# Down product and output projection with tokens on the partitions, read straight from PSUM

## The chip, the cores and the metric

The kernel runs on one core of a Trainium2 chip. The metric is the device time of one execution in microseconds, the median of the runs shown. Everything else comes from one profiled execution of the kernel before.

## The reference

The input is x, 32 sequences of 256 tokens with C = 128 channels, all in fp32. Three sublayers follow each other:

```
x = x + 0.5 * ffn(layernorm(x))
x = x + mamba(layernorm(x))
x = x + 0.5 * ffn(layernorm(x))

ffn(x):   router = x @ Wg; the top 2 of 8 experts, softmax weights w
          y  = sum over experts e of w[e] * (silu(x @ W1[e]) * (x @ W2[e])) @ W3[e]      (hidden 176)
          y += (silu(x @ Ws1) * (x @ Ws2)) @ Ws3                                         (hidden 352)
mamba(x): x_in, z = split(x @ W_in + b_in)            (256 inner channels each)
          xc = silu(causal conv of 4 taps over x_in + conv_b)
          B, C = split(xc @ W_xp + b_xp)              (16 states)
          delta = softplus(xc @ W_dt + b_dt)
          h_t = exp(delta_t * A) * h_(t-1) + delta_t * xc_t * B_t;  y_t = sum over states h_t * C_t + D * xc_t
          out = (y * silu(z)) @ W_out + b_out
          r = x + out;  return alpha * (r - mean(r)) / (std(r) + 1e-6) + beta
```

The residual inside `mamba` is its own input, that is the normalised x, so this normalised x is needed twice: as the input of `W_in` and, later, as the residual of the output projection.

## The kernel before, in words

Work goes in groups of two sequences, 512 tokens (TG), four tiles of 128 (TILES); there are G = 16 groups. A software pipeline of iterations k = -2 to 17 works on three groups at a time: in iteration k the first FFN runs for group k + 2, the projections that feed the scan for group k + 1, the scan itself for group k, the end of the mamba layer and the routing of the second FFN for group k - 1, and the second FFN for group k - 2. Each iteration has 32 slots. Every engine walks through the same slots in order and runs what the tables put there, so an instruction that waits holds back everything behind it on its engine. Hand-overs are semaphores.

In each slot: the scan of one of 16 states takes two slots. On even slots TensorE spreads a row of B over the partitions (`row_b`, L1008), VectorE scans (L868) and GpSimd multiplies by a row of C (L569); on odd slots VectorE makes the next input term (`input_term`, L834), which needs the `row_b` of the next even slot. The FFNs have NCHUNK = 14 units of 128 hidden channels each: the second one (f = 1) starts them in slots 0 to 13, the first one (f = 0) in slots 14 to 27. A unit is the up products `h1` and `h2` on TensorE (L1030, L1048), Silu on ScalarE (L680), the gate on VectorE one slot later (L860), for expert units another product on GpSimd (L521), and the down product four slots later (L1043) into the bank `ps_y`. The down product has `down_w` as the stationary operand and 512 tokens moving, so the channels come out on the partitions, `ps_y[c, token]`. The residual `xres` is kept with tokens on the partitions. So the result makes a detour: `y0`/`y1` copies `ps_y` to `yT` on ScalarE (L730), `yT0`/`yT1` transposes it in four blocks into the shared bank `ps_m` (L1079), and `addy0`/`addy1` adds half of it to `xres` on VectorE (L926). The first down product of the next FFN (slot 18 for f = 0, slot 4 for f = 1) waits until `ps_y` is taken (`y_taken`, L1042).

The output projection takes the same way: `outproj` (L1110) gives channels on the partitions, ScalarE adds `b_out` and copies to `oT` (L733), `outT` transposes, and `resid` (L961) adds it to `rtok` on VectorE. `rtok` holds the normalised residual: `x1n` (L699 to L706) computes it a second time on ScalarE, one iteration after `norm2` computed the same values for the projection. `stats3`, `ln_norm` and three GpSimd operations then finish the layer (`mamba_added`, L557).

All these small steps share one bank, `ps_m`. The order of their turns is the order in `PLAN` (L54): `claim` (L985) lets TensorE write only when the step before has been taken, and the taker is the engine that reads it: ScalarE for transposes of x, `in0` to `in3`, `dt0`, `dt1`, `bT`, `cT`, `wT`; VectorE for `logits`, `xproj`, `yT`, `outT`.

Other steps that matter: `gate_y` (L945) finishes the scan's output on VectorE; `weights0`/`weights1` (L908) turn the router's choice into weights, starting with `den` (L912); `wT0`/`wT1` transpose them, and SP writes them to memory and spreads them over the partitions again (`store_w`, `rows_w`). `delta` (L928) needs the softplus that ScalarE makes of `dt0`, `dt1` with Abs, Exp and Ln; `bparts` (L935) splits B into three bf16 parts. `SP_PLAN` (L64) is the same table for the DMA queue of SP.

## Time and profile before

| | |
|---|---|
| time, three runs | 2228.62, 2232.82, 2250.01 us; median 2232.82 |
| the profiled execution | 2241.29 us, its span 2239.5 us |
| mean granted clock of TensorE | 0.887 |
| TensorE busy | 1794.9 us, 80% of the span |
| VectorE busy | 1639.6 us, 73% |
| ScalarE busy | 1535.3 us, 69% |
| GpSimd busy | 1441.3 us, 64% |
| chain that ended last | PE 43%, ACT 21%, DVE 17%, issue 12%, POOL 3% |

PE is TensorE, PEld its weight loads, DVE VectorE, ACT ScalarE, POOL GpSimd; L numbers are lines of the kernel. A busy TensorE is not one at its full rate: the same instruction takes twice as long when the granted clock is at its lower level. Busy times of two instructions that follow each other can overlap by some hundredths of a microsecond; for the pace, read from start to start. An fp32 matmul shows as two records.

### The profile page before, as it was taken

To read this page: it belongs to the slowest core of one execution; us is meant where nothing else is said; L and a number is where in the kernel's file an instruction comes from. 1 tells how busy PE (TensorE), PEld (TensorE's weight loads), DVE (VectorE), ACT (ScalarE), POOL (GpSimd) and SP (SyncE) were. 2 spreads that over 40 slices of the span, in tenths; PEclk is the share of its full clock that TensorE was granted. 3 is DMA by queue.
4 is the path that set the end of the run, shared out by engine and by line. 5 is a ranking of instruction groups with operands and counts; after the bars stand their busy time and mean duration, and the time that the engine had idled before them with its cause. 6 is when DMAs were issued, how large, how long until landed. Compare 5 with 4: busy or idle time off the path is not lost.

```text
span 2239.5 us, 22836 instructions
## 1 busy us (share of the span) xinstructions
PE 1794.9 (80%) x4674; PEld 804.4 (36%) x4674; DVE 1639.6 (73%) x2505; ACT 1535.3 (69%) x2083; POOL 1441.3 (64%) x1286
## 2 busy tenths in 40 slices
PE   3878587979888888887888798788888878885577
PEld 1433233434334333333433343333333433332233
DVE  2257878687786878878687877878778786879742
ACT  1257587777778767786876778687677867776522
POOL 3346676666667675776767666676766676676753
PEclk9989788989898898998989898898989889897698
DMA  4117565555556555555555654655556555557642
GB/s 130 45 55 178 119 164 130 144 133 143 127 142 153 130 135 134 152 132 151 152 137 129 152 143 127 151 147 140 130 131 159 131 145 138 133 122 173 150 111 61
DMA packets 119129, 300.05 MB, mean 134 GB/s; under 512 B 19184, under 2 KB 40400, under 8 KB 104656
## 3 DMA queue, kind: packets, MB, share of 16 engines
q0 software_dynamic: 18432, 125.84, 28.1%
q1 hardware_dynamic: 92672, 168.88, 24.2%
q10 hardware_dynamic: 7888, 4.09, 0.7%
q14 instruction: 123, 1.01, 0.1%
q8 instruction: 14, 0.23, 0.0%
HBM read 167.67 MB, written 5.24 MB: 77 GB/s over the span
## 4 chain that ended last, share of the span: by engine, by line
PE 43%; ACT 21%; DVE 17%; issue 12%; POOL 3%; ACTq 1%; DMA 1%; DVEq 0%; POOLq 0%
PE ps_y L1043 9%; PE ps_h2a L1048 6%; DVE hist L868 5%; PE ps_m L1003 5%; ACT L680 5%; PE ps_h1a L1030 4%; PE ps_h1b L1030 4%; ACT L657 4%; PE ps_h2b L1048 4%; DVE den L912 3%; ACT decay L657 3%; ACT silu L680 2%; DVE yacc L950 2%; PE ps_m L1110 2%; DVE ps_db L834 2%
## 5 line engine op out<-in xcount | busy, mean ns | idle before, releaser
L569 POOL TENSOR_TENSOR prod<-hist,crow 128x1024 f32<-128x1024 f32 x224 | 556.0, 2482 | 371.8 <-DVE hist L868 368.0
L1043 PE MATMUL ps_y<-gated,down_w 128*128 128x512 f32 (+1 forms) x896 | 517.6, 664 | 101.3 <-POOL gated L521 63.2
L868 DVE TENSOR_TENSOR_SCAN hist<-decay,ps_db 128x1024 f32<-128x1024 f32 x256 | 583.2, 2278 | 13.8 <-issue 11.3
L521 POOL TENSOR_TENSOR gated<-gated,silu 128x512 f32<-128x512 f32 x352 | 476.3, 1416 | 138.1 <-DVE gated L860 108.4
L834 DVE TENSOR_TENSOR ps_db<-du,ps_db 128x1024 f32<-128x1024 f32 x256 | 313.7, 1225 | 319.1 <-PE ps_db L1012 318.8
L657 ACT ACTIVATE decay<-delta,a_neg 128x510 f32<-128x510 f32 x512 | 338.1, 711 | 2.6
L1048 PE MATMUL ps_h2a<-xnT,up_w 128*128 128x512 f32 (+1 forms) x448 | 253.2, 649 | 53.3 <-DVE gated L860 53.3
L680 ACT ACT_TABLE_LOAD x227 | 291.2, 1283 | 5.5 <-issue 0.7
L1043 PEld LDWEIGHTS ps_y<-gated,down_w 128*128 128x128 f32 (+1 forms) x896 | 180.3, 209 | 319.3 <-issue 218.0
L1030 PE MATMUL ps_h1a<-xnT,up_w 128*128 128x512 f32 (+1 forms) x448 | 248.0, 636 | 49.7 <-ACT silu L680 48.8
L657 ACT ACT_TABLE_LOAD x217 | 278.4, 1283 | 3.8
L1030 PE MATMUL ps_h1b<-xnT,up_w 128*128 128x512 f32 x448 | 240.1, 618 | 38.8 <-ACT silu L680 38.5
L1048 PE MATMUL ps_h2b<-xnT,up_w 128*128 128x512 f32 x448 | 235.9, 609 | 0.0
L680 ACT ACTIVATE silu<-ps_h1a 128x512 f32<-128x512 f32 (+1 forms) x224 | 132.8, 593 | 57.6 <-PE ps_h1a L1030 57.3
L680 ACT ACTIVATE silu<-ps_h1b 128x512 f32<-128x512 f32 x224 | 133.8, 597 | 48.3 <-PE ps_h1b L1030 43.1
L1012 PE MATMUL ps_db<-bT,sel_b 96*128 96x512 bf16 x256 | 108.3, 423 | 69.4 <-DVE hist L868 69.3
L860 DVE TENSOR_TENSOR gated<-ps_h2b,wrow 128x512 f32<-128x512 f32 x192 | 131.2, 683 | 41.2 <-PE ps_h2b L1048 41.2
L860 DVE TENSOR_TENSOR gated<-ps_h2a,wrow 128x512 f32<-128x512 f32 x160 | 108.5, 678 | 68.2 <-PE ps_h2a L1048 64.8
L1048 PEld LDWEIGHTS ps_h2a<-xnT,up_w 128*128 128x128 f32 (+1 forms) x448 | 89.0, 202 | 183.0 <-issue 109.8
L718 ACT ACTIVATE bounce<-ps_m 8x512 f32<-8x512 f32 x32 | 18.8, 587 | 184.7 <-PE ps_m L993 184.7
L1030 PEld LDWEIGHTS ps_h1b<-xnT,up_w 128*128 128x128 f32 x448 | 81.4, 196 | 134.7 <-issue 69.2
L1003 PE MATMUL ps_m<-xnT,w_conv 128*128 128x512 f32 (+3 forms) x256 | 121.9, 621 | 6.6 <-DVE rtok L961 4.2
(137 smaller groups left out, 2242.5 us busy)
## 6 DMA issues: line engine op xcount, KB each, us to landing
yacc<-prod POOLq DMA_DIRECT2D x112, 1024.0 KB, 9.0
crow<-c_rows SPq DMA_DIRECT2D x128, 512.0 KB, 4.2
wrow<-w_rows SPq DMA_DIRECT2D x320, 128.0 KB, 3.6
wrow<-w_rows SPq DMA_DIRECT2D x64, 224.0 KB, 3.2
wrow<-w_rows SPq DMA_DIRECT2D x64, 192.0 KB, 3.6
wrow<-w_rows SPq DMA_DIRECT2D x64, 160.0 KB, 3.4
yacc<-yacc POOLq DMA_DIRECT2D x16, 512.0 KB, 6.2
wrow<-w_rows SPq DMA_DIRECT2D x64, 96.0 KB, 3.3
```

What stands on the lines that cost most here:

```text
L521: nc.gpsimd.tensor_tensor(gated[:, pos % NGATE, :], gated[:, pos % NGATE, :], silu[:, (pos + NCHUNK * f_parity(k, f)) % NSILU, :], ALU.mul ...
L569: nc.gpsimd.tensor_tensor(prod[:, (pair - 1 + odd) % 2, s % 2, :, :], hist[:, s % 2, :, :], c_all, ALU.mult).then_inc(prod_done, 1)
L657: ins = nc.scalar.activation(decay[:, s % NA, half, :, 1:LEN], d[:, :, 1:LEN], ACT.Exp, scale=a_neg[:, half, s:s + 1])
L680: nc.scalar.activation(silu[0:r, (pos + NCHUNK * f_parity(k, f)) % NSILU, :], ps_h1[pos % 2][0:r, :], ACT.Silu).then_inc(silu_done, 1)
L834: nc.vector.tensor_tensor(ps_db[:].rearrange("p (h t) -> p h t", h=HALVES), du[par][:], ps_db[:, TG:2 * TG].unsqueeze(1).to_broadcast([P, ...
L860: nc.vector.tensor_tensor(gated[0:r, pos % NGATE, :], ps_h2[pos % 2][0:r, :], factor, ALU.mult).then_inc(h2_taken, 1)
L868: nc.vector.tensor_tensor_scan(hist[:, s % 2, :, :].rearrange("p h t -> p (h t)"), decay[:, s % NA, :, :, :].rearrange("p h b t -> p (h b ...
L1003: nc.tensor.matmul(acc[:, :, late:LEN], w_conv[:, tap, half * P:(half + 1) * P], now[:, :, 0:LEN - late], start=(tap == PAD), stop=False)
L1012: nc.tensor.matmul(ps_db[:, TG:2 * TG], sel_b[:, s, :], bT[par][:], start=True, stop=True).then_inc(b_full, 1)
L1030: nc.tensor.matmul(ps_h1[pos % 2][0:r, :], up_w[:, 0, j * P:j * P + r], xnT[f][:], start=True, stop=True).then_inc(h1_full, 1)
L1043: nc.tensor.matmul(ps_y[:], down_w[0:rd, jd, :], gated[0:rd, posd % NGATE, :], start=(posd == 0), stop=(posd == NCHUNK - 1)).then_inc(down ...
L1048: nc.tensor.matmul(ps_h2[pos % 2][0:r, :], up_w[:, 1, j * P:j * P + r], xnT[f][:], start=True, stop=True).then_inc(h2_full, 1)
```

## The change

The operands of two products are swapped. In the down product each of the four token tiles of `gated` is the stationary operand, and the 128 columns of `down_w` move; the result has tokens on the partitions. `addy` reads `ps_y` itself and sets `y_taken`; `y0`, `y1`, `yT0`, `yT1` and `yT` are gone. The output projection is turned in the same way, with the bias brought in first by a matmul of a row of ones with `b_out`; `resid` reads its result, `outT` and `oT` are gone. `norm2` writes into one of two kept tiles, `x1n[2]`, and SP copies it to `rtok` with a DMA in slot 17 (`keep_x1n`); the second computation is gone. Most steps of `PLAN` and some of `SP_PLAN` get new slots.

```diff
-        0: ["stats0", "y0"], 1: ["yT0", "x1n"], 2: ["addy0", "norm0"], 3: ["stats2", "fold"], 4: ["xT0"],
-        5: ["logits0", "norm2"], 6: ["route0", "gate_y"], 7: ["xT2"], 8: ["weights0", "outproj"], 9: ["in0"],
-        10: ["wT0"], 11: ["outT"], 12: ["resid"], 13: ["in1", "stats3"], 14: ["in2"],
-        15: ["in3", "ln_norm"], 17: ["y1"], 18: ["dt0", "stats1"], 19: ["dt1"], 20: ["yT1", "norm1"],
-        21: ["addy1"], 22: ["xproj", "delta"], 23: ["bparts"], 24: ["xT1"], 25: ["logits1"], 26: ["route1"],
-        27: ["cT"], 28: ["bT", "weights1"], 30: ["wT1"],
+        0: ["stats0", "addy0"], 1: ["stats2"], 2: ["norm0"], 3: ["norm2", "fold"], 4: ["xT0"], 5: ["logits0"],
+        6: ["route0", "xT2"], 7: ["gate_y"], 8: ["weights0"], 9: ["outproj"], 10: ["resid", "in0", "stats3"],
+        11: ["wT0"], 12: ["in1"], 13: ["in2"], 14: ["in3", "ln_norm"], 16: ["dt0"], 17: ["dt1", "addy1", "stats1"],
+        19: ["xproj", "norm1"], 20: ["delta", "bparts"], 21: ["xT1"], 22: ["logits1"], 23: ["route1"],
+        24: ["cT"], 25: ["weights1"], 26: ["bT"], 28: ["wT1"],
     }
     UP1, UP0, BACK = 0, 14, 4
 
     SP_PLAN = {
         0: ["c1"], 3: ["c2"], 4: ["w1:4"], 5: ["w1:5"], 6: ["w1:6"], 7: ["c3", "w1:7"], 8: ["w1:8"], 9: ["w1:9"],
-        10: ["w1:10"], 11: ["store_w0", "c4"], 12: ["w0:0"], 13: ["w0:1"], 14: ["w0:2"], 15: ["w0:3", "c5"],
-        18: ["w0:4"], 19: ["c6", "w0:5"], 20: ["w0:6"], 21: ["w0:7"], 22: ["store_x", "w0:8"], 23: ["c7", "w0:9"],
-        24: ["w0:10"], 28: ["next_c0"], 30: ["store_w1", "w1:0", "w1:1", "w1:2", "w1:3"],
+        10: ["w1:10"], 11: ["c4"], 12: ["store_w0"], 13: ["w0:0", "w0:1"], 14: ["w0:2"], 15: ["w0:3", "c5"],
+        17: ["keep_x1n"], 18: ["w0:4"], 19: ["c6", "w0:5"], 20: ["w0:6"], 21: ["store_x", "w0:7"], 22: ["w0:8"],
+        23: ["c7", "w0:9"], 24: ["w0:10"], 28: ["next_c0"], 29: ["store_w1", "w1:0", "w1:1", "w1:2", "w1:3"],
     }
 
...
-    MISC_LEAD = ["yT0", "xT2", "in0", "in1", "in2", "in3", "dt0", "dt1", "xproj", "cT", "bT"]
-    MISC_TAIL = ["outproj", "outT", "xT1", "logits1", "wT1"]
-    MISC_LAST = ["yT1"]
+    MISC_LEAD = ["xT2", "in0", "in1", "in2", "in3", "dt0", "dt1", "xproj", "cT", "bT"]
+    MISC_TAIL = ["outproj", "xT1", "logits1", "wT1"]
...
+        b_out_r = sb("b_out_r", [1, C])
+        ones_r = sb("ones_r", [1, P])
...
-        xn = [sb(f"xn{f}", [P, TILES, C]) for f in range(2)]
-        xn = [xn[0], xn[0], xn[1]]
+        xn = sb("xn", [P, TILES, C])
+        x1n = [sb(f"x1n{i}", [P, TILES, C]) for i in range(2)]
...
@@ -369,7 +366,7 @@
 
             def store(g, slot, first, k):
 
-                sp.wait_ge(misc_taken, turn(k, "yT1"))
+                sp.wait_ge(y_taken, ffn_no(k, 1) + 1)
...
+                        elif step == "keep_x1n" and scans(k):
+                            sp.wait_ge(norm_ready[2], k + 1)
+                            if tail(k):
+                                sp.wait_ge(mamba_added, k)
+                            sp.dma_start(rtok[:], x1n[odd][:]).then_inc(x1n_ready, 16)
...
                         elif step == "stats2" and lead(k):
                             if tail(k):
-                                pool.wait_ge(x1n_ready, k)
+                                pool.wait_ge(norm_ready[2], k)
                             scale_and_bias(k, step, mv1[:, nxt, :, :], ln_eps, rstd1[:, nxt, :],
                                            nbias1[:, nxt, :], k + 2)
...
+                const(b_out_r[:], b_out.rearrange("(o c) -> o c", o=1))
...
-                            normalise(xn[0], xres[:, entering, :, :], nbias[0], rstd[0]).then_inc(norm_ready[0], 1)
+                            normalise(xn, xres[:, entering, :, :], nbias[0], rstd[0]).then_inc(norm_ready[0], 1)
                         elif step == "norm1" and tail(k):
                             plain_wait()
                             act.wait_ge(nbias_ready[1], k)
-                            normalise(xn[1], xres[:, behind, :, :], nbias[1], rstd[1]).then_inc(norm_ready[1], 1)
+                            normalise(xn, xres[:, behind, :, :], nbias[1], rstd[1]).then_inc(norm_ready[1], 1)
                         elif step == "norm2" and lead(k):
                             plain_wait()
+                            if tail(k):
+                                act.wait_ge(x1n_ready, 16 * k)
                             act.wait_ge(nbias_ready[2], k + 2)
-                            normalise(xn[2], xres[:, ahead, :, :], nbias1[:, nxt, :], rstd1[:, nxt, :]
+                            normalise(x1n[nxt], xres[:, ahead, :, :], nbias1[:, nxt, :], rstd1[:, nxt, :]
                                       ).then_inc(norm_ready[2], 1)
-                        elif step == "x1n" and tail(k):
-
-                            plain_wait()
-                            act.wait_ge(nbias_ready[2], k)
-                            if not isinstance(k, int) or k > 1:
-                                act.wait_ge(mamba_added, k - 1)
-                            normalise(rtok, xres[:, behind, :, :], nbias1[:, nxt, :], rstd1[:, nxt, :]
-                                      ).then_inc(x1n_ready, 1)
...
-                        elif step == "y0" and lead(k) or step == "y1" and last(k):
-                            f = int(step[1])
-                            act.wait_ge(down_done, fcount(k if f else k - 1, f, NCHUNK, NCHUNK))
-                            nc.scalar.activation(yT[:], ps_y[:], ACT.Copy).then_inc(y_taken, 1)
-                        elif step == "outproj" and tail(k):
-                            take(k, step)
-                            nc.scalar.activation(oT[:], ps_m[:], ACT.Identity,
-                                                 bias=b_out_c[:, 0:1]).then_inc(misc_taken, 1)
                         elif step in ("in0", "in1") and lead(k):
                             half = int(step[2])
+                            if tail(k):
+                                act.wait_ge(yg_ready, k)
                             take(k, step)
                             nc.scalar.activation(xconv[nxt][:, half, :], ps_m[:], ACT.Silu,
                                                  bias=b_conv[:, half:half + 1]).then_inc(misc_taken, 1)
@@ -880,7 +871,7 @@
                             statistics(xres[:, behind, :, :], 1, mv[1], stats_no(k, 1))
...
-                            dve.wait_ge(misc_taken, turn(k, "yT0"))
+                            dve.wait_ge(y_taken, ffn_no(k - 1, 0) + 1)
                             statistics(xres[:, ahead, :, :], 2, mv1[:, nxt, :, :], stats_no(k, 2))
...
                         elif step == "addy0" and lead(k) or step == "addy1" and last(k):
                             f = int(step[4])
-                            dve.wait_ge(misc_full, turn(k, f"yT{f}"))
+                            dve.wait_ge(down_done, fcount(k if f else k - 1, f, NCHUNK, NCHUNK))
                             xr = xres[:, oldest if f else ahead, :, :].rearrange("p t c -> p (t c)")
-                            nc.vector.scalar_tensor_tensor(xr, ps_m[:], 0.5, xr, ALU.mult, ALU.add
-                                                           ).then_inc(misc_taken, 1)
+                            nc.vector.scalar_tensor_tensor(xr, ps_y[:], 0.5, xr, ALU.mult, ALU.add
+                                                           ).then_inc(y_taken, 1)
...
                         elif step == "resid" and tail(k):
-                            dve.wait_ge(x1n_ready, k)
-                            dve.wait_ge(misc_full, turn(k, "outT"))
+                            dve.wait_ge(x1n_ready, 16 * k)
+                            dve.wait_ge(misc_full, turn(k, "outproj"))
                             r2 = rtok[:].rearrange("p t c -> p (t c)")
                             nc.vector.tensor_tensor(r2, r2, ps_m[:], ALU.add).then_inc(misc_taken, 1)
                         elif step == "stats3" and tail(k):
                             plain_wait()
-                            dve.wait_ge(misc_taken, turn(k, "outT"))
+                            dve.wait_ge(misc_taken, turn(k, "outproj"))
                             statistics(rtok, 3, mvr, stats_no(k, 3))
...
                         if posd == 0 and (not isinstance(k, int) or k > -2):
                             pe.wait_ge(y_taken, ffn_no(k, fd))
-                        nc.tensor.matmul(ps_y[:], down_w[0:rd, jd, :], gated[0:rd, posd % NGATE, :], start=(posd == 0),
-                                         stop=(posd == NCHUNK - 1)).then_inc(down_done, 1)
+                        for t in range(TILES):
+                            ins = nc.tensor.matmul(ps_y[:, t * C:(t + 1) * C],
+                                                   gated[0:rd, posd % NGATE, t * P:(t + 1) * P], down_w[0:rd, jd, :],
+                                                   start=(posd == 0 and t == 0),
+                                                   stop=(posd == NCHUNK - 1 and t == TILES - 1))
+                        ins.then_inc(down_done, 1)
...
                             pe.wait_ge(norm_ready[f], (k + 3, k, k + 2)[f])
                             claim(k, step)
-                            to_rows(xn[f], P, ident, ps_m).then_inc(misc_full, 1)
+                            to_rows(x1n[nxt] if f == 2 else xn, P, ident, ps_m).then_inc(misc_full, 1)
...
-                        elif step == "yT0" and lead(k) or step == "yT1" and last(k):
-                            f = int(step[2])
-                            pe.wait_ge(y_taken, ffn_no(k if f else k - 1, f) + 1)
-                            claim(k, step)
-                            to_rows(yT, P, ident, ps_m).then_inc(misc_full, 1)
...
                         elif step == "outproj" and tail(k):
                             pe.wait_ge(yg_ready, k)
                             claim(k, step)
-                            for half in range(HALVES):
-                                ins = nc.tensor.matmul(ps_m[:], w_out[:, half, :], yacc[nxt][:, 0, half, :],
-                                                       start=(half == 0), stop=(half == HALVES - 1))
+                            nc.tensor.matmul(ps_m[:].rearrange("p (t c) -> p t c", t=TILES), ones_r[:],
+                                             b_out_r[:].unsqueeze(1).to_broadcast([1, TILES, C]), start=True,
+                                             stop=False)
+                            for t in range(TILES):
+                                for half in range(HALVES):
+                                    ins = nc.tensor.matmul(ps_m[:, t * C:(t + 1) * C],
+                                                           yacc[nxt][:, 0, half, t * P:(t + 1) * P],
+                                                           w_out[:, half, :], start=False,
+                                                           stop=(t == TILES - 1 and half == HALVES - 1))
                             ins.then_inc(misc_full, 1)
-                        elif step == "outT" and tail(k):
-                            claim(k, step)
-                            to_rows(oT, P, ident, ps_m).then_inc(misc_full, 1)
```

## Rows read from the trace of the kernel before

**Rows 1.** Window view of one iteration: busy us per engine (instructions), clock, DMA.
```profile
1018.99:1149.62 130.63, 110.29 (x294) 49.44 (x293) 103.83 (x156) 99.98 (x135) 89.94 (x80) 0.90 0.55 142
```

**Rows 2.** TensorE's timeline, same iteration: start, us, instructions; idle before and its releaser.
```profile
1023.43 0.65 PE L993 MATMUL ps_m<-ident,yT 128*128 128x128 f32 x4 [0.76 <-ACT yT L730]
...
1027.91 1.35 PE L1030 MATMUL ps_h1b<-xnT,up_w 128*128 128x512 f32 x2 [1.89 <-ACT silu L680]
...
1051.10 1.13 PE L1048 MATMUL ps_h2a<-xnT,up_w 128*128 128x512 f32 x2 [3.68 <-DVE gated L860]
...
1056.35 3.58 PE L1003 MATMUL ps_m<-xnT,w_conv 128*128 128x512 f32 x8
...
1092.49 1.10 PE L1043 MATMUL ps_y<-gated,down_w 128*128 128x512 f32 x2 [3.17 <-ACT yT L730]
1093.43 1.80 PE L1048 MATMUL ps_h2a<-xnT,up_w 128*128 128x512 f32 x2
1095.02 2.84 PE L1093 MATMUL ps_m<-xconv,w_dt 128*128 128x512 f32 x4
...
1111.57 2.08 PE L1030 MATMUL ps_h1a<-xnT,up_w 128*128 128x512 f32 x2 [3.19 <-ACT silu L680]
...
1139.80 2.08 PE L1043 MATMUL ps_y<-gated,down_w 128*128 128x512 f32 x2 [3.75 <-POOL gated L521]
```

**Rows 3.** Summary of TensorE's waits, whole run: us, times, longest.
```profile
PE ps_y L1043 <- ACT yT L730: 38.0, 12, 3.2
```

**Rows 4.** TensorE's timeline, back to back at full clock.
```profile
1044.88 0.60 PE L993 MATMUL ps_m<-ident,xn 128*128 128x128 f32 x4
1045.32 0.38 PE L1012 MATMUL ps_db<-bT,sel_b 96*128 96x512 bf16 x1
1045.54 1.02 PE L1030 MATMUL ps_h1a<-xnT,up_w 128*128 128x512 f32 x2
1046.39 1.02 PE L1043 MATMUL ps_y<-gated,down_w 128*128 128x512 f32 x2
```

**Rows 5.** TensorE's timeline, an x-projection at full clock.
```profile
217.41 1.87 PE L1102 MATMUL ps_m<-w_xp,xconv 128*128 128x32 f32 x16
219.12 1.10 PE L1030 MATMUL ps_h1b<-xnT,up_w 128*128 128x512 f32 x2
```

**Rows 6.** Groups by line and shape: busy us, mean ns, idle before, releaser.
```profile
L868 DVE TENSOR_TENSOR_SCAN hist<-decay,ps_db 128x1024 f32<-128x1024 f32 x256 | 583.2, 2278 | 13.8 <-issue 11.3
...
L834 DVE TENSOR_TENSOR ps_db<-du,ps_db 128x1024 f32<-128x1024 f32 x256 | 313.7, 1225 | 319.1 <-PE ps_db L1012 318.8
...
L860 DVE TENSOR_TENSOR gated<-ps_h2b,wrow 128x512 f32<-128x512 f32 x192 | 131.2, 683 | 41.2 <-PE ps_h2b L1048 41.2
...
L912 DVE TENSOR_SCALAR den<-edrop 128x4 f32<-128x4 f32 x32 | 73.4, 2294 | 1.0 <-POOL edrop L542 1.0
...
L933 DVE TENSOR_TENSOR du<-delta,xconv 128x1024 f32<-128x1024 f32 x16 | 50.1, 3130 | 0.5
...
L914 DVE TENSOR_TENSOR prob<-edrop,prob 128x4 f32<-128x4 f32 x32 | 36.1, 1128 | 1.1
...
L819 DVE CAST bparts<-bc 128x64 bf16<-128x64 f32 x16 | 25.2, 1577 | 0.5
...
L644 ACT ACTIVATE rtok<-xres,nbiasx,rstdx 128x128 f32 x48 | 19.6, 483 | 0.0
...
L730 ACT ACTIVATE yT<-ps_y 128x512 f32<-128x512 f32 x32 | 18.9, 591 | 19.9 <-PE ps_y L1043 19.9
```

**Rows 7.** VectorE's timeline, same iteration.
```profile
1027.96 0.69 DVE L860 TENSOR_TENSOR gated<-ps_h2b,silu 128x512 f32<-128x512 f32 x1 [2.18 <-ACT silu L680]
...
1039.92 1.23 DVE L834 TENSOR_TENSOR ps_db<-du,ps_db 128x1024 f32<-128x1024 f32 x1 [2.21 <-PE ps_db L1012]
...
1139.00 5.51 DVE L912 TENSOR_SCALAR den<-edrop 128x4 f32<-128x4 f32 x1
```

**Rows 8.** DMA issues: KB each, median us to landing.
```profile
out<-xres SPq DMA_DIRECT2D x16, 256.0 KB, 2.9
```

9 lines of the change are left out of this document (3 added, 6 removed).

## The prediction

> **What bounds the kernel now.** I read the window view of one whole iteration first [rows 1]. It lasts 130.6 us and is one of the 12 (k = 2 to 13) that hold every step. TensorE is busy for 110 of it, VectorE for 104, ScalarE for 100, so three engines are nearly full and a freed engine soon meets the next. The granted clock is 0.90, so TensorE spends part of the time at the lower level. Next I read TensorE's own timeline through that iteration [rows 2]: where it waits, and for whom. It waits for ScalarE in the head (0.76 before `yT0`'s transposes, 1.89 before an up matmul), for VectorE in slot 8 (3.68), not at all from there to slot 18, then for the eviction `yT` (3.17), then for a Silu behind the Exp/Ln chain (3.19), and in the tail for GpSimd (3.75). These six come to 16.4 us. The summary of waits has the `yT` one 12 times, 38.0 us in all [rows 3], so every full iteration has it.
>
> A wait costs more than its length. After 3.19 us of idling the next two-record matmul takes 2.08 instead of 1.02 [rows 2, 4], the lower of the two levels (1.2 instead of 2.4 GHz); after 3.17 us the next but one takes 1.80, and the four records of dt0 2.84, where at the full rate four last 4 x 0.43 + 0.16 = 1.88.
>
> **The matmuls turned round.** Before, a down unit is two records of 512 moving columns, 0.86 from start to start (1045.54 to 1046.39 is such a pair [rows 4]). After, it is four tiles of two records, each with 128 moving columns of `down_w` and its own load of 128 columns of `gated`: eight loads and eight short matmuls. Columns moved are the same, 0.86 us. The question is whether the loads hide. The nearest rows: the x-projection already has this form with 32 columns, and its 16 records take 1.71 us (217.41 to 219.12, and the pair behind them lasts 1.10, so this is the full clock [rows 5]), 107 ns each, so a 128-column fp32 load passes in at most 107 ns. The fp32 transposes load 128 columns and move 128, and four take 0.44 (1044.88 to 1045.32 [rows 4]), 110 ns each, so load and movement overlap there. Hence 8 x 107 to 8 x 110 = 0.86 to 0.88: I take no change, upper bound load and movement in series, 8 x 214 = 1.71 us, lower bound 0.86.
>
> The Trainium skill speaks against this change: its page "TensorE: Matmul & The Clock Gate" (Back-to-back issue gap) gives about 81 ns for each matmul of 128 columns in a stream of load and matmul pairs, against 56 ns without loads. By that ratio, an estimate, a down unit would take 1.24 us, 10.7 us more in an iteration. The transposes do not show it (110 ns with a 128-column load), but they are not quite the same instruction.
>
> The output projection goes from four records (1.72) to sixteen of 128 columns (16 x 107 = 1.71) plus the bias matmul of 512 columns (0.86). Removed are `outT`, `yT0`, `yT1`, 0.44 each. TensorE's net is -0.5 us an iteration, bounds -0.5 and +25.
>
> **What leaves the other queues.** ScalarE loses three evictions of a bank, two `yT` at 0.59 and `oT` (taken alike), and `x1n`, four instructions of 0.48 [rows 6]: 1.8 + 1.9 = 3.7 us. VectorE loses nothing: the residual add reads the other bank at the same size. The copy of x1n is one 256 KB transfer on SP in slot 17; the output transfer of the same size takes 2.9 us [rows 8]. Its readers come in slot 10 of the next iteration, so I cost it at nothing. It waits for `mamba_added`, and behind it on SP stand `w0:4` and `c6`, wanted from slot 19; before, GpSimd's last add ends before VectorE's statistics in slot 18 need it, so that cover holds. Were it late by one 2.9 us transfer, the rows of weights would be too.
>
> **Now the schedule, stretch by stretch,** in us per iteration.
> (a) Slot 18. `y_taken` now comes from VectorE's add in slot 17 (as long as a gate, 0.68 [rows 6]), with dt1 (1.72) and an up matmul (0.86) of TensorE's between: no wait. Gain 3.17, and the slow passage behind it (1.80 for 1.02, 2.84 for 1.88 [rows 2]), 1.7: **-4.9**. Bounds 0 and -4.9. The Silu wait of 3.19 stays: its chain of Abs, Exp, Ln and their table loads moves two slots but keeps its length.
> (b) Head, slots 0 to 8. ScalarE's `yT` and `x1n` go, 0.59 + 1.93 = 2.5 us, and `wT1` reaches it two slots sooner; its two waits are worth 2.7, and smaller ones follow. VectorE is late next: in this stretch it is idle only 2.18 + 2.21 = 4.4 [rows 7]. I take **-3.3**, bounds 0 and -4.4. The move of `gate_y` behind the gate of slot 7 lies inside this.
> (c) Tail. `den` of weights1 stood in slot 28 for 5.51 us [rows 7] on four elements a partition, so nearly all of it is a wait inside the instruction; no up unit covers it there, and scan 15, the first weights of the next iteration and the clock all wait. It moves to slot 25. Scan 14 to the next row_b then is GpSimd's and VectorE's pace: **-5.3**, bounds -2 and -6.
> (d) TensorE's content: **-0.5**.
> (e) Slot 10. `resid` and `in0` now share slot and bank, so the convolution waits for VectorE's add, which stands behind input term 1.23, gate 0.68 and scan 2.28, and is as long as a gate [rows 6]: 4.9 after row_b, 4.6 with overlaps. TensorE's own slot is 0.22 + 3 x 0.86 = 2.8. That alone is a wait of 1.8; and without in0 in slot 9 (3.58 [rows 2]) TensorE comes 3.6 sooner, less 0.1, while VectorE is still held by `gate_y` and weights0. Wait 5.3, slow passage 0.8 (3.17 us lowered the clock, 3.68 did not): **+6.1**, bounds +1.8 and +9.
> (f) Slots 20 to 22. du (3.1) and the parts of B (the first cast alone 1.6 [rows 6]) stand in one slot with a scan, 7.0 us of VectorE against 2.8 of TensorE; xT1 waits for `bc` and the gates stand behind: **+3.2**, bounds 0 and +5.
> (g) Slot 25. weights1 costs on average 2.3 + 1.1 for `den` and `prob` [rows 6] and 1.0 for the rest, 4.4 us of VectorE; some 2.4 has slack: **+2.0**, bounds 0 and +4.4.
> Similar waits in slot 6 (xT2 behind route0, 2 us) fall where VectorE sets the pace anyway: 0.
>
> Sum -14.0 + 11.3 = **-2.7 us**. The sixteen iterations that scan, twelve of them full, give -43; the four at the ends lose a hop of 0.59 + 0.44 and two handovers, 1.5 each, -6. The profiled execution took 2241.3 us (span 2239.5), 8.5 above the median of the three runs; 2241.3 - 49 = 2192, or **2184** on the median's scale.
>
> **Rivals.**
> *New waits do not bind* (0.20). VectorE runs ahead as ScalarE feeds it sooner, and (e) to (g) cost about half, 6, with the rest as is: -14 + 6 = -8, x 16 and the -6 of the ends, 2099. For it: ScalarE, busy 100 of 130.6, has its idle time in the tail behind `wT1`, and that moves; against: VectorE too has only 4.4 idle in the head.
> *Nothing is left* (0.15). Either (e) to (g) eat all, or a short record takes 120 ns: 28 x 8 x 13 ns = +2.9 an iteration, 2233.
> *Slower: in0 behind resid* (0.13). The price is in slot 10. If the clock falls in the wait and stays down over in0, that is 5.3 + 3.7, and (a) gives back only its 3.17: -2.7 + 2.9 + 1.7 + some 1.5 more in (f) = +3.4, 16 x 3.4 = +54, 2285. It decides as soon as TensorE stands more than about 5 us there in most iterations.
> *Slower: loads not hidden* (0.07). If a load and a movement of 107 ns follow each other, 28 x 0.85 = +24 an iteration, +380, near 2570; if they overlap by half, near 2380. The 110 ns of the transposes speak against it [rows 4]. (By the ratio of the Trainium skill's page it would be 16 x 10.7 = +171, near 2355.)
> *The forecast* (0.45): small gain, 2150 to 2215.
>
> **Numbers.** A measurement of this kernel tells about 1% (22 us) from no change. Faster by over 1% means below 2210: 0.20 + nearly all of 0.45 less 0.04, 0.61. Within 1%: 0.15 + 0.04, 0.19. Slower: 0.13 + 0.07, 0.20. The range leaves out the 0.07, half of the 0.13 and a quarter of the 0.20: 2090 to 2275.
>
> **What would show it.** Down records near 107 ns at full clock, and 0.86 for a unit, or the loads rival is true. No wait at slot 18 and no `den` of 5 us in the tail, for (a) and (c). A wait of 4 to 6 us before the first convolution, released by `rtok`, for (e); if it is under 2, the second case holds. ScalarE 3.7 us less busy an iteration. A mean clock at or above 0.89; below 0.87 the slot 10 rival holds. Most likely wrong are the sizes of (e) and (f), because they depend on how far VectorE is behind.

## The result and the profile after

The kernel after takes 2350.11 us (median of four runs, 2347.12 to 2353.02) against 2234.21 (2228.62 to 2250.01) of the kernel before: a ratio of 1.0507, interval 1.0451 to 1.0562. It is 116 us slower, where 2184 was forecast, and lies outside the range. The profiled execution took 2351.95 us, its mean granted clock is 0.882.

The page of the kernel after (span 2350.2 us): busy time by engine, a queue that carries instructions, and the chain that ended last.

```profile
PE 1850.3 (79%) x7394; PEld 1087.3 (46%) x7394; DVE 1647.8 (70%) x2505; ACT 1484.2 (63%) x1973; POOL 1437.7 (61%) x1287
...
q8 instruction: 67, 1.10, 0.2%
...
PE 39%; DVE 25%; issue 14%; ACT 9%; POOL 9%; DMA 2%; ACTq 1%; DVEq 1%; POOLq 0%
```

ScalarE is 51 us less busy than before, 3.2 an iteration, nearly the 3.7 that the prediction counted. VectorE and GpSimd are busy as before to within 8 us. So the work did leave, and the time still grew. TensorE is busy 55 us longer, in part at the lower clock and in part with the slightly longer down units (13 us, priced under e8), and the other 55 us of the longer span are its waits. The queue q8 (packets, MB, share) had 14 packets and 0.23 MB before.

The window view of two iterations, which answers to [rows 1] (window, length, busy us of PE, PEld, DVE, ACT, POOL with instructions, clock, DMA share, GB/s):

```profile
922.35:1058.69 136.34, 113.72 (x463) 67.27 (x463) 102.08 (x155) 96.20 (x126) 87.74 (x77) 0.91 0.52 130
1058.69:1199.67 140.98, 114.56 (x463) 67.41 (x462) 105.85 (x158) 96.34 (x126) 91.14 (x82) 0.90 0.55 141
```

Both are longer than the 130.6 of before, at 0.91 and 0.90 of the clock against 0.90. They differ from each other because the program's loop runs over two iterations, and one of the two has the wait at the loop's end (4.67, told of below; the difference is 4.64).

TensorE's timeline, a full-clock passage of the first and then the second of these iterations, which answers to [rows 2, 4] (start, us, instructions; idle before and its releaser):

```profile
1008.00 1.05 PE L1035 MATMUL ps_y<-down_w,gated 128*128 128x128 f32 x8
1008.89 1.02 PE L1043 MATMUL ps_h2a<-xnT,up_w 128*128 128x512 f32 x2
...
1092.56 1.12 PE L1043 MATMUL ps_h2b<-xnT,up_w 128*128 128x512 f32 x2 [2.89 <-DVE gated L851]
1093.61 2.07 PE L1099 MATMUL ps_m<-b_out_r,ones_r 1*128 1x512 f32 x2
1095.61 3.78 PE L1104 MATMUL ps_m<-w_out,yacc 128*128 128x128 f32 x16
...
1104.51 3.68 PE L994 MATMUL ps_m<-xnT,w_conv 128*128 128x512 f32 x8 [1.72 <-DVE rtok L952]
...
1137.34 1.55 PE L1035 MATMUL ps_y<-down_w,gated 128*128 128x128 f32 x8 [3.67 <-POOL gated L524]
1138.68 1.91 PE L1043 MATMUL ps_h2b<-xnT,up_w 128*128 128x512 f32 x2
1140.38 2.37 PE L1083 MATMUL ps_m<-xconv,w_dt 128*128 128x512 f32 x4
1142.59 0.38 PE L1003 MATMUL ps_db<-bT,sel_b 96*128 96x512 bf16 x1
```

Four things are to be seen. A turned down unit takes 0.89 from start to start at full clock (1008.00 to 1008.89), so the loads hide. The wait for `yT` (3.17 before) is gone, but in slot 17, one slot ahead of where it was, stands one of 3.67 for GpSimd's last gate product. The output projection runs at the lower clock, 3.78 us for its sixteen records, behind a wait of 2.89 for VectorE in slot 8, where 3.68 stood before with a projection at full clock behind it. And the convolution waits 1.72 for `resid`, not 5.3.

The summary of waits of the kernel after (engine, tile, line, releaser: us, times, longest), which answers to [rows 3]:

```profile
PE ps_y L1035 <- POOL gated L524: 126.6, 59, 7.1
...
PE ps_h2b L1043 <- DVE gated L851: 64.9, 29, 2.9
PE ps_m L994 <- DVE rtok L952: 27.7, 14, 4.2
...
PE ps_h1a L1021 <- issue: 18.2, 5, 4.7
```

Before, the first of these was 63.2 us in 21 waits; now it is 63.4 us more in 38 more waits. The last line is of another kind and is told of below.

Why is GpSimd late? Its own timeline around slots 14 to 17 of the same iteration, kernel after:

```profile
1127.99 1.26 POOL L553 TENSOR_TENSOR rtok<-rtok,alpha_b 128x512 f32<-128x512 f32 x1 [7.09 <-ACT rtok L647]
...
1132.07 2.35 POOL L572 TENSOR_TENSOR prod<-hist,crow 128x1024 f32<-128x1024 f32 x1
...
1135.09 0.89 POOL L589 DMA_DIRECT2D yacc<-prod  x1 [0.24 <-issue]
1135.70 1.58 POOL L524 TENSOR_TENSOR gated<-gated,silu 128x512 f32<-128x512 f32 x1
```

And the same stretch of the kernel before, with the gate product first:

```profile
1083.82 1.59 POOL L521 TENSOR_TENSOR gated<-gated,silu 128x512 f32<-128x512 f32 x1
1086.90 1.27 POOL L550 TENSOR_TENSOR rtok<-rtok,alpha_b 128x512 f32<-128x512 f32 x1 [1.49 <-ACT rtok L644]
```

`ln_norm` moved from slot 15 to 14. In each slot GpSimd's program has the gate product first, then the steps of the table, then the product of the scan, so a step that moves from slot 15 to 14 passes ahead of slot 15's gate product. GpSimd now comes to it too soon, stands 7.09 us for ScalarE's part of it, then owes three operations, the product of slot 14's scan and a DMA issue, 7.71 us together (1127.99 to 1135.70), and only then the gate product for which TensorE has waited 3.67. Over the run GpSimd waits 106.1 us for this release in the kernel after, 20.7 before. TensorE's wait of this slot is there in twelve iterations (3.67 to 3.70 each), and a thirteenth has 7.13.

### The profile page after: what moved, and what is told of

Same layout as the page of the kernel before. It is cut to its first block, busy times and chain, and to the rows that moved or that the text cites. A ratio compares the mean times of both kernels' runs of the same rounds, so it can differ in the third digit from the quotient of the medians.

```text
span 2350.2 us, 28083 instructions
## 1 busy us (share of the span) xinstructions
PE 1850.3 (79%) x7394; PEld 1087.3 (46%) x7394; DVE 1647.8 (70%) x2505; ACT 1484.2 (63%) x1973; POOL 1437.7 (61%) x1287
## 4 chain that ended last, share of the span: by engine, by line
PE 39%; DVE 25%; issue 14%; ACT 9%; POOL 9%; DMA 2%; ACTq 1%; DVEq 1%; POOLq 0%
DVE hist L859 10%; PE ps_y L1035 8%; PE ps_m L994 5%; PE ps_h2b L1043 5%; PE ps_h1a L1021 4%; POOL gated L524 4%; POOL prod L572 4%; PE ps_h1b L1021 3%; DVE ps_db L825 3%; PE ps_h2a L1043 3%; PE ps_m L1104 2%; DVE gated L851 2%; DVE yacc L941 2%; ACT L683 2%; ACT L660 2%
## 5 line engine op out<-in xcount | busy, mean ns | idle before, releaser
L572 POOL TENSOR_TENSOR prod<-hist,crow 128x1024 f32<-128x1024 f32 x224 | 549.3, 2452 | 327.3 <-DVE hist L859 326.1
L1035 PEld LDWEIGHTS ps_y<-down_w,gated 128*128 128x128 f32 (+1 forms) x3584 | 506.7, 208 | 347.8 <-POOL gated L524 192.7
L1035 PE MATMUL ps_y<-down_w,gated 128*128 128x128 f32 (+1 forms) x3584 | 528.3, 296 | 128.6 <-POOL gated L524 126.6
L524 POOL TENSOR_TENSOR gated<-gated,silu 128x512 f32<-128x512 f32 x352 | 487.4, 1452 | 137.9 <-DVE gated L851 127.3
L1043 PE MATMUL ps_h2b<-xnT,up_w 128*128 128x512 f32 x448 | 250.5, 643 | 65.0 <-DVE gated L851 64.9
L1021 PE MATMUL ps_h1a<-xnT,up_w 128*128 128x512 f32 (+1 forms) x448 | 254.6, 652 | 32.8 <-issue 18.2
L1043 PE MATMUL ps_h2a<-xnT,up_w 128*128 128x512 f32 (+1 forms) x448 | 241.9, 623 | 7.3 <-DVE gated L851 6.3
L994 PE MATMUL ps_m<-xnT,w_conv 128*128 128x512 f32 (+3 forms) x256 | 130.3, 657 | 33.5 <-DVE rtok L952 27.7
L1021 PEld LDWEIGHTS ps_h1a<-xnT,up_w 128*128 128x128 f32 (+1 forms) x448 | 89.4, 205 | 91.7 <-issue 63.6
L729 ACT ACTIVATE xconv<-ps_m,b_conv 128x512 f32<-128x512 f32 x32 | 22.0, 687 | 160.8 <-PE ps_m L996 160.8
```

The source lines that it names most:

```text
L524: nc.gpsimd.tensor_tensor(gated[:, pos % NGATE, :], gated[:, pos % NGATE, :], silu[:, (pos + NCHUNK * f_parity(k, f)) % NSILU, :], ALU.mul ...
L572: nc.gpsimd.tensor_tensor(prod[:, (pair - 1 + odd) % 2, s % 2, :, :], hist[:, s % 2, :, :], c_all, ALU.mult).then_inc(prod_done, 1)
L994: nc.tensor.matmul(acc[:, :, late:LEN], w_conv[:, tap, half * P:(half + 1) * P], now[:, :, 0:LEN - late], start=(tap == PAD), stop=False)
L1021: nc.tensor.matmul(ps_h1[pos % 2][0:r, :], up_w[:, 0, j * P:j * P + r], xnT[f][:], start=True, stop=True).then_inc(h1_full, 1)
L1035: ins = nc.tensor.matmul(ps_y[:, t * C:(t + 1) * C], gated[0:rd, posd % NGATE, t * P:(t + 1) * P], down_w[0:rd, jd, :], start=(posd == 0 a ...
L1043: nc.tensor.matmul(ps_h2[pos % 2][0:r, :], up_w[:, 1, j * P:j * P + r], xnT[f][:], start=True, stop=True).then_inc(h2_full, 1)
```

## The experiments

The theories at the start: the loss comes from the two steps that moved in slots 9 to 15 (`ln_norm`, and `resid` with `in0`); or it comes from the short records of the turned products; or from the new head or the new tail. Each experiment changes one of these. All times are medians against the kernel before on the same chip, which took 2238.64 us beside e1 to e4, 2232.81 beside e5 to e8, 2235.12 beside e9 to e11 and 2246.2 beside e12. Two kernels measured beside different ones are therefore known against each other to a few microseconds only; where it matters, the ratios to before are given too.

**The products alone, in the old slots (e1_old_slots).** The kernel after with the slots of before (the cut shows the table of before, then e1's): `addy0` in 0, `addy1` in 17, `outproj` in 11, the detours left out, the copy of x1n in slot 17.

```diff
-        0: ["stats0", "y0"], 1: ["yT0", "x1n"], 2: ["addy0", "norm0"], ... 8: ["weights0", "outproj"],
-        ... 11: ["outT"], 12: ["resid"], ... 17: ["y1"], ... 20: ["yT1", "norm1"], 21: ["addy1"],
+        0: ["stats0", "addy0"], 2: ["norm0"], ... 8: ["weights0"],
+        ... 11: ["outproj"], 12: ["resid"], ... 17: ["addy1"], ... 20: ["norm1"],
```

> The changed kernel's products, kept x1n and copy, in the slots of the kernel before: only addy0 moves to slot 0, addy1 to slot 17 and the output projection to slot 11, where outT stood. Placement theory (the slots 9 to 17 of the new table lose the time): no wait of 3.7 us for GpSimd before the last down product, no wait of the first convolution for rtok; some 138 us per iteration fall to 128 to 131, the time is 2190 to 2250 us. Product theory (eight short records with their own loads lose it, through the loads or the longer loop body): still above 2300 us, because all short records stay.

Measured 2191.63 us, ratio 0.9796 (0.975 to 0.9842), 47 us faster than before, at the lower end of the range that was expected (2190 to 2250). So turning the products, with the x1n kept, is no loss. All that the kernel after loses, 159 us from here, lies in its tables of slots, `PLAN` and `SP_PLAN`. TensorE's timeline of this kernel at slots 17 and 18 and further on:

```profile
1069.32 1.88 PE L1125 MATMUL ps_m<-xconv,w_dt 128*128 128x512 f32 x4
1071.04 1.02 PE L1063 MATMUL ps_h1b<-xnT,up_w 128*128 128x512 f32 x2
1071.89 1.05 PE L1077 MATMUL ps_y<-down_w,gated 128*128 128x128 f32 x8
...
1084.91 1.35 PE L1063 MATMUL ps_h1a<-xnT,up_w 128*128 128x512 f32 x2 [3.25 <-ACT silu L725]
```

No wait of 3 us is left there; the Silu wait behind it stays (3.25 here, 3.19 in [rows 2]), as forecast.

**The down product wide again, rest as after (e2_wide_down).** This kernel leaves out what the wide form needs: `ps_y` holds channels on the partitions and is added to `xres` as it stands, without transposes. It serves to price the records.

```diff
-                        for t in range(TILES):
-                            ins = nc.tensor.matmul(ps_y[:, t * C:(t + 1) * C],
-                                                   gated[0:rd, posd % NGATE, t * P:(t + 1) * P], down_w[0:rd, jd, :],
-                                                   start=(posd == 0 and t == 0),
-                                                   stop=(posd == NCHUNK - 1 and t == TILES - 1))
-                        ins.then_inc(down_done, 1)
+                        nc.tensor.matmul(ps_y[:], down_w[0:rd, jd, :], gated[0:rd, posd % NGATE, :], start=(posd == 0),
+                                         stop=(posd == NCHUNK - 1)).then_inc(down_done, 1)
```

> The changed kernel, but each down unit is again one matmul of 512 moving columns (two records), with down_w stationary; ps_y then holds channels on the partitions and is added to xres untransposed, so the output is not the reference's. Everything else, slots too, is as in the changed kernel. Placement theory: only the 0.03 us per unit (0.89 against 0.86 us, 13 us in all) and the waits of 2.4 to 4.7 us at the end of a pass of TensorE's loop (5 seen, with the slow passage some 25 us) go: 2305 to 2330 us. Product theory: most of the 116 us goes, below 2270 us.

Measured 2339.4 us, 1.0468 (1.0421 to 1.0515): 11 us less than after, where 20 to 45 were expected. The short records are not the cause of the 116 us. They cost less here than the 30 us that e8 finds for them; where the rest went was not followed.

**ln_norm back in slot 15 (e3_lnnorm_15).**

```diff
-        11: ["wT0"], 12: ["in1"], 13: ["in2"], 14: ["in3", "ln_norm"], 16: ["dt0"], ...
+        11: ["wT0"], 12: ["in1"], 13: ["in2"], 14: ["in3"], 15: ["ln_norm"], 16: ["dt0"], ...
```

> The changed kernel with one step moved: ln_norm from slot 14 to slot 15, where it stood before, so that GpSimd's product for the last down unit (issued in slot 15 ahead of the table's steps) does not stand behind its three operations. Placement theory: TensorE's wait of 3.67 us before the down product of slot 17 and the slow passage behind it go or shrink to under 1 us: 3 to 5 us per iteration, 2270 to 2305 us. Product theory: within 1% of 2350 us.

Measured 2274.1 us, 1.016 (1.0111 to 1.021): 76 us less than after, for one step moved by one slot. Its GpSimd timeline, where the gate product comes first again, and TensorE's down product of slot 17, without a wait:

```profile
1109.28 1.59 POOL L546 TENSOR_TENSOR gated<-gated,silu 128x512 f32<-128x512 f32 x1
1111.86 1.27 POOL L575 TENSOR_TENSOR rtok<-rtok,alpha_b 128x512 f32<-128x512 f32 x1 [0.99 <-ACT rtok L669]
```

```profile
1112.82 1.05 PE L1057 MATMUL ps_y<-down_w,gated 128*128 128x128 f32 x8
```

In its summary of TensorE's waits, the one for GpSimd's gate product is back to the size of before (63.2 us in 21 waits):

```profile
PE ps_y L1057 <- POOL gated L546: 62.6, 34, 5.1
```

**The order of slots 9 to 15 as before (e4_resid_12).** `in0` in 9, `wT0` 10, `outproj` 11, `resid` 12, `in1` and `stats3` 13, `in2` 14, `in3` and `ln_norm` 15; the rest as after.

```diff
-        9: ["outproj"], 10: ["resid", "in0", "stats3"], 11: ["wT0"], 12: ["in1"], 13: ["in2"], 14: ["in3", "ln_norm"],
+        9: ["in0"], 10: ["wT0"], 11: ["outproj"], 12: ["resid"], 13: ["in1", "stats3"], 14: ["in2"],
+        15: ["in3", "ln_norm"],
```

> The changed kernel with only the slots 9 to 15 laid out as before: in0 9, wT0 10, outproj 11, resid 12, in1 and stats3 13, in2 14, in3 and ln_norm 15; the head (0 to 8) and the tail (16 to 28) keep the new slots. Placement theory: the first convolution no longer waits for rtok and the wait for GpSimd in slot 17 is gone; 2250 to 2290 us, and what is still above the old-slot kernel is what the new head and tail cost. Product theory: above 2320 us.

Measured 2210.51 us, 0.9881 (0.9837 to 0.9925): 64 us less than e3, 140 less than after, and below the range that was expected (2250 to 2290). The wait for `rtok` is down from 25.4 us in 14 waits (e3) to 4.2 in one.

**The place of stats3 (e5_stats3_13).** e3 with `stats3` in slot 13. In e3 and in the kernel after GpSimd stands in slot 10 for these statistics (5.20 us in the kernel after), ahead of its products; this run asks whether that costs the 64 us.

```diff
-        10: ["resid", "in0", "stats3"], 11: ["wT0"], 12: ["in1"], 13: ["in2"],
+        10: ["resid", "in0"], 11: ["wT0"], 12: ["in1"], 13: ["in2", "stats3"],
```

> The kernel of e3_lnnorm_15 (2274 us) with only stats3 moved from slot 10 to slot 13, so that GpSimd no longer stands 5.2 us in slot 10 waiting for these statistics in front of the products of the scan and the gates; resid and in0 stay together in slot 10. Theory A (the convolution behind the residual add, and the slow passage after the wait of 2.9 us before the output projection, cost the rest): no change, 2265 to 2285 us. Theory B (GpSimd's early wait costs it): most of the 64 us down to e4_resid_12 goes, 2215 to 2240 us.

Measured 2278.55 us, 1.0203 (1.0144 to 1.0263), as e3. GpSimd's wait for these statistics falls from 88.7 us in the whole run (e3) to 2.6, and the time does not follow: it is not that.

**The tail alone (e6_new_tail).** e1 with slots 16 to 31 of the new table, and SP's from slot 21.

```diff
-        17: ["addy1"], 18: ["dt0", "stats1"], 19: ["dt1"], 20: ["norm1"], 22: ["xproj", "delta"], 23: ["bparts"],
-        24: ["xT1"], 25: ["logits1"], 26: ["route1"], 27: ["cT"], 28: ["bT", "weights1"], 30: ["wT1"],
+        16: ["dt0"], 17: ["dt1", "addy1", "stats1"], 19: ["xproj", "norm1"], 20: ["delta", "bparts"], 21: ["xT1"],
+        22: ["logits1"], 23: ["route1"], 24: ["cT"], 25: ["weights1"], 26: ["bT"], 28: ["wT1"],
```

> The kernel of e1_old_slots (2192 us) with slots 16 to 31 as in the changed kernel (dt0 16, dt1 and stats1 17, xproj and norm1 19, delta and bparts 20, xT1 21, logits1 22, route1 23, cT 24, weights1 25, bT 26, wT1 28, and SP's table from slot 21). The prediction's terms (c), (f) and (g) together are -5.3 + 3.2 + 2.0 = -0.1 us per iteration: 2180 to 2200 us. Rival (the crowding of VectorE and ScalarE in slots 19 to 22 costs more than the emptied tail gives): 2200 to 2215 us. If den's wait in the tail was worth its 5 us: below 2150 us.

Measured 2183.93 us, 0.9789 (0.9727 to 0.9851), 8 us below e1, 2 by the ratios: the new tail is worth little, and whether anything is not shown. This is the lowest time of a version that computes everything; e11, at 2185.54, can't be told from it, and e1 by the ratios can't either.

**The head alone (e7_new_head).** e1 with slots 0 to 8 of the new table.

```diff
-        2: ["norm0"], 3: ["stats2", "fold"], 4: ["xT0"], 5: ["logits0", "norm2"], 6: ["route0", "gate_y"], 7: ["xT2"],
+        1: ["stats2"], 2: ["norm0"], 3: ["norm2", "fold"], 4: ["xT0"], 5: ["logits0"], 6: ["route0", "xT2"],
+        7: ["gate_y"],
```

> The kernel of e1_old_slots with slots 0 to 8 as in the changed kernel (stats2 1, norm2 3, xT2 6 beside route0, gate_y 7). The prediction took this head for worthless or slightly good (the wait of xT2 for route0 falls where VectorE sets the pace): 2180 to 2195 us. Rival (each wait counts): TensorE waits 1.58 for route0 and 2.9 behind gate_y instead of once 3.58, +0.9 us and a slow passage per iteration: 2200 to 2215 us.

Measured 2213.31 us, 0.9909 (0.9881 to 0.9938), 22 us above e1 (25 by the ratios). The two waits of slots 6 to 8, as the kernel after has them, come with it. Its summary, then e1's:

```profile
PE ps_h2b L1086 <- DVE gated L894: 41.1, 15, 2.9
...
PE ps_m L1027 <- DVE logit L923: 30.7, 16, 3.8
```

```profile
PE ps_h2a L1085 <- DVE gated L893: 52.8, 16, 3.8
...
PE ps_m L1026 <- DVE logit L922: 11.5, 3, 3.8
```

The two are not alike. The wait for the gate in slot 8 is no new one: with the 6.9 us of `ps_h2a` it comes to 48.0 in e7, less than the 52.8 of e1. The wait for `logit`, where the transpose of x1n now stands in the slot of `route0`, is new in 13 iterations and is 19 us more; the waits for VectorE's scan (`hist`) rise by another 14 (85.9 to 99.6). TensorE's busy time does not grow (1778.7 against 1781.5).

Even so, the wait of 2.89 has a cause worth seeing. One instruction of VectorE is stretched. Groups of VectorE by shape (busy us, mean ns, idle), first the kernel after, then the same line of before:

```profile
L945 DVE TENSOR_TENSOR yacc<-yacc,zs 128x1024 f32<-128x1024 f32 x16 | 58.0, 3627 | 0.5
```

```profile
L954 DVE TENSOR_TENSOR yacc<-yacc,zs 128x1024 f32<-128x1024 f32 x16 | 19.6, 1225 | 0.6
```

The second operation of `gate_y` takes 3.63 us where it took 1.23. In the timelines of the kernel after, VectorE and then GpSimd:

```profile
1086.78 3.99 DVE L945 TENSOR_TENSOR yacc<-yacc,zs 128x1024 f32<-128x1024 f32 x1
```

```profile
1086.87 2.81 POOL L524 TENSOR_TENSOR gated<-gated,silu 128x512 f32<-128x512 f32 x2
```

VectorE's begins as GpSimd takes up two gate products, which end at 1089.68, and ends 1.1 later, about its own length. The `den` of before is alike: it ran from 1139.00 for 5.51 us, four elements a partition, and GpSimd's products ended at 1144.47. In both cases an operation of VectorE that reads and writes SBUF alone stood until GpSimd's run of operations ended. The Trainium skill's page "SBUF — State Buffer" (SBUF: two separate sides) gives a rule for it: a VectorE operation with two SBUF inputs and a GpSimd operation that reads SBUF share a port pair under an exclusive lock, and the second one blocks. The trace agrees for `gate_y` in that one of the two stands; VectorE's record begins 0.09 us ahead of GpSimd's and it stood all the same, through two products and not one. `den` has a single tensor operand; the page counts operations in a two-port mode as well, and no run here shows whether it is one.

**Wide down product in the old slots (e8_wide_down_old).** The edit of e2 made to e1; it leaves out the transposes as e2 does.

```diff
-                        for t in range(TILES):
...
+                        nc.tensor.matmul(ps_y[:], down_w[0:rd, jd, :], gated[0:rd, posd % NGATE, :], start=(posd == 0),
```

> The kernel of e1_old_slots with each down unit again one matmul of 512 columns, down_w stationary (ps_y then holds channels on the partitions and is added untransposed, so the output is not the reference's). It prices the short records where TensorE is busiest: 0.03 us x 28 x 16 = 13 us plus five loop waits of about 4 us with their slow passages, if nothing hides them 2150 to 2165 us; if they hide as in the changed kernel (11 us there) 2175 to 2185 us.

Measured 2161.53 us, 0.968 (0.9623 to 0.9737), 30 us below e1 (26 by the ratios): here the short records do cost. Two terms give it. A unit takes 0.89 and not 0.86: 0.03 x 28 x 16 = 13 us. And TensorE stands at the loop's end. The summary's line for it, of e1 and then of e8:

```profile
PE ps_h1a L1063 <- issue: 20.2, 5, 4.3
```

```profile
PE ps_h1a L1063 <- issue: 1.0, 5, 0.2
```

Together 13 + 19 = 32 us, measured 30.

**A slot between resid and in0 (e9_in0_11).** e3 with `in0` in slot 11 and the steps behind it up to `in3` one later, to size the wait itself; SP's store of the first weights moves one slot too, to 13.

```diff
-        10: ["resid", "in0", "stats3"], 11: ["wT0"], 12: ["in1"], 13: ["in2"], 14: ["in3"], 15: ["ln_norm"],
+        10: ["resid", "stats3"], 11: ["in0"], 12: ["wT0"], 13: ["in1"], 14: ["in2"], 15: ["in3", "ln_norm"],
```

> The kernel of e3_lnnorm_15 (2274 us) with one slot put between the residual add and the first convolution: outproj 9, resid and stats3 10, in0 11, wT0 12, in1 13, in2 14, in3 and ln_norm 15. TensorE has a whole slot (2.7 us) of other work in front of the claim. Theory A (the wait for rtok, 1.7 to 2.1 us an iteration, is what this placement costs): the wait goes, -27 to -35 us, 2240 to 2248 us; what is left above e4_resid_12 (2210 us) belongs to the output projection standing right behind the wait of 2.9 us and running at the lower clock level. Theory B (nearly all is the projection's slow passage): 2265 to 2275 us. Theory C (all of it is the wait and what follows it): 2210 to 2225 us.

Measured 2248.55 us, 1.0055 (1.003 to 1.0079): 26 us less than e3 (23 by the ratios). TensorE's waits for `rtok` fall from 25.4 us in 14 to 4.8 in two, 20.6 less. The other 38 us that e4 gives are not this wait. TensorE's timelines show two parts of them. e9:

```profile
1051.87 1.62 PE L1084 MATMUL ps_h2b<-xnT,up_w 128*128 128x512 f32 x2 [2.89 <-DVE gated L892]
1053.42 2.07 PE L1140 MATMUL ps_m<-b_out_r,ones_r 1*128 1x512 f32 x2
1055.42 3.78 PE L1145 MATMUL ps_m<-w_out,yacc 128*128 128x128 f32 x16
...
1074.02 1.16 PE L1076 MATMUL ps_y<-down_w,gated 128*128 128x128 f32 x8 [1.38 <-POOL gated L565]
```

and e4:

```profile
1036.34 5.27 PE L1016 MATMUL ps_m<-xnT,w_conv 128*128 128x512 f32 x8
...
1047.84 1.12 PE L1121 MATMUL ps_m<-b_out_r,ones_r 1*128 1x512 f32 x2
1048.89 2.05 PE L1126 MATMUL ps_m<-w_out,yacc 128*128 128x128 f32 x16
```

Behind the 2.89 wait, what comes next runs wholly or in part at the lower level (before, the projection behind 3.68 did not, so the length of the wait alone does not tell). In e9 that is the up matmul (1.55 from start to start, 0.96 in e4) and the bias and output projection (5.57, against 2.94); in e4 it is the convolution (5.21, against 3.51 in e9). Then e9 has a wait for GpSimd in slot 12 (1.38) that e4 hasn't. 0.59 + 2.63 - 1.70 + 1.38 = 2.9, which in twelve to fourteen iterations makes 35 to 41 us. This sum is read off one iteration of each trace. Over the run the wait for GpSimd is 20.4 us more in e9 (78.0 in 47 waits against 57.6 in 36) and TensorE is busy 11.8 us longer, 32 of the 38. No run isolates a part of it, so those 38 us are explained and not shown.

**x1n computed twice (e10_x1n_twice).** e1 with the second computation on ScalarE in slot 1, as before, and no copy.

```diff
+        1: ["x1n"],
...
-        17: ["keep_x1n"],
```

> The kernel of e1_old_slots (2192 us), but x1n is again computed a second time on ScalarE in slot 1 straight into rtok (four instructions of 0.48), and the copy on SP is gone. It prices the kept x1n and its transfer. If ScalarE sets the pace of the head, as the prediction held: +1.0 to +2.0 us an iteration, 2208 to 2224 us. Rival (VectorE sets it there, or the transfer costs as much as it saves): within 8 us of 2192.

Measured 2203.74 us, 0.9857 (0.9793 to 0.992), 12 us above e1 (14 by the ratios), between the two ranges that were expected, with 1508.5 us of ScalarE against 1483.9. Keeping the tile is worth some 12 us, less than the 16 to 32 that ScalarE would give if it set the pace of the head; the transfer costs nothing that shows.

**One FFN turned, one not (e11_half_turned).** e6, the down product of f = 0 wide, with its detour `y0`, `yT0`, `addy0` in slots 0, 1 and 2; f = 1 and the output projection turned.

```diff
-        0: ["stats0", "addy0"],
-        2: ["norm0"],
+        0: ["stats0", "y0"],
+        1: ["yT0"],
+        2: ["addy0", "norm0"],
...
+                        if not fd:
+                            ins = nc.tensor.matmul(ps_y[:], down_w[0:rd, jd, :], gated[0:rd, posd % NGATE, :],
+                                                   start=(posd == 0), stop=(posd == NCHUNK - 1))
```

> The kernel of e6_new_tail (2184 us), with the down product turned only for the second FFN (f = 1), whose eviction stood in the way of slot 18; for the first FFN it is one matmul of 512 columns again, with the eviction y0 in slot 0, the four transposes yT0 in slot 1 and the add from the shared bank in slot 2. Half of the short records go: -7 us of TensorE, and the loop body is shorter by 168 pairs of load and matmul. If the waits at the end of the loop come with the length of the body, they shrink or go, -10 to -18 us; the detour costs ScalarE 0.59 and TensorE 0.44 an iteration in the head, +5 to +15 us. Together 2160 to 2190 us; if the head is ScalarE's, above 2190 us.

Measured 2185.54 us, 0.9786 (0.9724 to 0.9847), as e6. The wait at the loop's end was expected to shrink if it went with the length of the loop; it stays (16.1 us in 5, 14.7 in e6), though 1280 of the 7394 matmuls are gone. For f = 0, whose detour lies in the head and not at slot 18, turning neither gains nor loses.

**ln_norm in slot 14, in the kernel before (e12_before_ln14).**

```diff
-        10: ["wT0"], 11: ["outT"], 12: ["resid"], 13: ["in1", "stats3"], 14: ["in2"],
-        15: ["in3", "ln_norm"], 17: ["y1"], ...
+        10: ["wT0"], 11: ["outT"], 12: ["resid"], 13: ["in1", "stats3"], 14: ["in2", "ln_norm"],
+        15: ["in3"], 17: ["y1"], ...
```

> The kernel before, unchanged but for one step: ln_norm moves from slot 15 to slot 14. No product is turned. Placement theory (in slot 14 GpSimd waits for ScalarE's ln_norm and runs three operations ahead of the scan's product of slot 14 and of the last gate's product of slot 15): a wait for GpSimd of 2 to 4 us appears before the down product of slot 17, then a slow passage; as in the changed kernel, where moving it back gave 76 us, +40 to +90 us, 2275 to 2325 us. Rival (the move hurts only together with the new slots of resid and stats3, which make ScalarE's ln_norm late): within 1%, 2215 to 2255 us.

Measured 2266.95 us, 1.0098 (1.0078 to 1.0119), 21 us slower, between the 40 to 90 that were expected and the rival's "within 1%". The same wait comes up in the same slot, and GpSimd's sequence ahead of it is as in the kernel after. TensorE, then GpSimd:

```profile
1093.43 2.07 PE L1043 MATMUL ps_y<-gated,down_w 128*128 128x512 f32 x2 [3.74 <-POOL gated L521]
```

```profile
1084.04 1.27 POOL L550 TENSOR_TENSOR rtok<-rtok,alpha_b 128x512 f32<-128x512 f32 x1 [2.83 <-ACT rtok L644]
...
1091.80 1.58 POOL L521 TENSOR_TENSOR gated<-gated,silu 128x512 f32<-128x512 f32 x1
```

It costs 21 and not 76 because before had its `yT` wait (3.17) in the very next slot, and that is not in this kernel's summary: the one took the other's place. The summaries add up: the waits for GpSimd's gate product rise from 63.2 to 120.0 us, the 38.0 for `yT` go, which leaves 19. So the gain of step (a) and the loss by `ln_norm` are the same three microseconds, first given back and then taken.

## Why the prediction was wrong

The steps add up along the chain of versions: before 2235, products and kept x1n in the old slots (e1) 2192, with the new tail (e6) 2184, with the new head as well (e4) 2211, with slots 9 to 14 as after but for `ln_norm` (e3) 2274, with `ln_norm` in slot 14 (after) 2350. Beside it the prediction's own terms, times its sixteen iterations:

| part | forecast, us | measured, us | between |
|---|---|---|---|
| products and kept x1n in the old slots: (a), (b), (d) and the ends | -145 | -43 | before, e1 |
| tail: (c), (f), (g) | -2 | -8 | e1, e6 |
| steps moved in the head | 0, inside (b) | +27 | e6, e4 |
| slots 9 to 14: (e) | +98 | +64 | e4, e3 |
| `ln_norm` one slot earlier | no term | +76 | e3, after |
| sum | -49 | +116 | |

No single step makes the miss of 165 us: the first row gave 102 too little, `ln_norm` cost 76, the head 27; (e), priced too high, hid 34 of it, and the tail 6.

- **The step that failed: (a), "no wait".** It looked at slot 18's `y_taken` alone, and by that it was right: e1 has no wait there. But the moved `ln_norm` was never priced on any engine, though it is four instructions of ScalarE and three of GpSimd, and moves past a gate product in GpSimd's queue. That is 76 of the 116 us (e3). From one iteration: a wait of 3.67, and behind it 1.34, 1.70 and 2.21 from start to start where 0.89, 0.86 and 1.72 are the full rate, 5.45 in all. Twelve iterations at that, and the thirteenth with its 7.13, are 74. e12 shows the same wait in the kernel before, with no other step moved.
- **(e) `in0` behind `resid`: the wait is real, its size a third.** Predicted +6.1 an iteration, 5.3 of it wait. Measured 64 us, 4.0 an iteration, but only 26 of them go with the wait (e9), which is 1.7 in this iteration; the rest sits in slots 8 and 12, for which (e) had no term. The wait is shorter, as far as one iteration tells, because the output projection behind slot 8's wait runs slowly (5.6 for bias and product where 2.6 is the full rate) and brings TensorE to slot 10 some 3 us later. The sign that the prediction gave for it, "if it is under 2, the second case holds", misled: 1.72 was read in this iteration, and the time had gone elsewhere.
- **(b) the head: a small gain, and the moves lose more.** Predicted -3.3 an iteration, -53 us, for a freed ScalarE. The kept x1n is worth 12 us (e10), and the detour of f = 0 nothing (e11). TensorE's waits for a Silu ahead of `h1b` do fall (38.5 to 11.4 us from before to e1), but those for VectorE's `hist` and `wtok` rise (69.3 to 85.9, 33.3 to 44.3): VectorE was next, as the prediction feared, and sooner. The moved steps then cost 22 us (e7). "Similar waits in slot 6 ... 0" was the error there: the transpose of x1n waits 1.6 for `route0`, 26.9 us in 15 waits in the kernel after. That `gate_y`'s move "lies inside this" held in so far as the wait of slot 8 only changed its instruction (3.68 before, 2.89 after), though its second operation now meets GpSimd's two gate products, 2.4 us more.
- **(c), (f), (g) the tail: right as a sum, (c) wrong by itself.** Predicted -5.3 + 3.2 + 2.0 = -0.1 an iteration; measured -8 us, -0.5, which is not clear of nothing (e6). The sum is right because two wrong sizes cancel, which is luck. (c) took the time inside `den` as gone once it moves. It went into the operations behind it. The groups of the same step in e1, then in e6:

```profile
L945 DVE TENSOR_SCALAR den<-edrop 128x4 f32<-128x4 f32 x32 | 73.6, 2299 | 1.0 <-POOL edrop L587 1.0
...
L947 DVE TENSOR_TENSOR prob<-edrop,prob 128x4 f32<-128x4 f32 x32 | 36.0, 1127 | 1.1
```

```profile
L946 DVE TENSOR_TENSOR prob<-edrop,prob 128x4 f32<-128x4 f32 x32 | 59.5, 1860 | 1.1
...
L944 DVE TENSOR_SCALAR den<-edrop 128x4 f32<-128x4 f32 x32 | 14.5, 453 | 1.4 <-POOL edrop L586 1.2
```

`den` gives up 59.1 us, 3.7 an iteration where (c), from the one `den` of 5.51, has 5.3. `prob` takes 23.5 of them back, and of the two operations behind it `hotp` 10.3 (22.6 to 32.9) and `wtok` 11.6 (6.1 to 17.7), so 14 are left. That (f) and (g) are smaller than forecast by as much follows from the sum only; no run took them apart. For (f) the groups show one reason: beside the new steps the cast of `bparts` takes 14.3 us in all and not 37.5, and `delta` 19.6 and not 27.4, so VectorE as a whole is 36 us less busy in e6 than in e1.

- **The products, (d) and the rival "loads not hidden".** 0.86 to 0.88 a unit was predicted, 0.89 measured, 111 ns a record. The rival is out, and with it the figure of the Trainium skill's page "TensorE: Matmul & The Clock Gate" (Back-to-back issue gap), by whose ratio a unit would take 1.24. What nobody priced is the loop's end: 18.2 us in the kernel after, 20.2 in e1, 14.7 to 23.7 in the other kernels with the short records.
- **The size of (a) with what belongs to it.** e8 against before is -71 us; less the 12 of the kept x1n (e10) that leaves some -59, for twelve to sixteen iterations of (a) at 4.9 and (d) at 0.5, 65 to 86. So this gain was there at nearly its size, at the twelve iterations in which the `yT` wait stood rather than the sixteen that the sum took, and the records and the loop's end took 30 of it. No run parts it from what the removed evictions give ScalarE.
- **The rivals.** "In0 behind resid" gave 2285, and e3, which has all of the change but the `ln_norm` move, stands at 2274. (By its own terms the rival comes to 2281, 6.1 an iteration above the forecast, as "nothing is left" with its +2.9 comes to 2230 and not 2233; neither changes a chance.) Its direction was the true one, and it had 0.13, but that the numbers lie close is luck: it asked for a stand of more than about 5 us ahead of `in0` with the convolution at the lower clock, and the wait was 1.72 with the convolution at full clock (3.68 us). Its sign, a mean clock below 0.87, did not come either (0.882).

The chain of waits itself is not a safe guide here. In the kernel after it names VectorE's scan as what came before the late gate product, since the scan ends just before the product starts (start, us, what):

```profile
1133.18 2.29 DVE hist L859
...
1135.70 1.59 POOL gated L524
```

But in e3 the same product starts at 1109.28, before VectorE's next scan begins (1110.96), so it doesn't need that scan. What is constant is the start 0.61 to 0.66 behind GpSimd's own DMA issue, in before, after, e3 and e12.

## What to carry to other kernels

When a table of steps changes, list for each moved step every engine that takes part in it and what it now passes in that engine's queue; one step moved by one slot cost 76 us here, on GpSimd, the least busy of the four engines. Check too in how many iterations a wait stands before multiplying it: the `yT` wait stood in 12, and the sum took 16. A wait removed is worth its length only if no other engine is late for the same instruction or the next: ask who is second before the gain is booked. Of two SBUF-to-SBUF operations, one of VectorE and one of GpSimd, only one seems to run at a time (two cases here, no run that isolates it), so the place of a long one against the other engine's bursts is part of its price.

## What the hardware showed that was not expected

- **TensorE stops where its loop turns.** The first matmul behind it stands for 2.1 to 5.2 us, for nothing that the profile shows, in the kernels with short down records, and at most 0.25 in those with wide ones alone. It comes in every second iteration, five times a run, where the program's loop, of two iterations, starts again. Of the kernel after:

```profile
1199.67 2.07 PE L1021 MATMUL ps_h1a<-xnT,up_w 128*128 128x512 f32 x2 [4.67 <-issue]
```

With it the queue q8, which carries instructions, moves 67 packets and 1.10 MB (64 and 1.05 MB in e11) against 14 and 0.23 MB in before and e8. A pass of the kernel after has 2 x 926 matmul and load records, one of before 2 x 587. The Trainium skill's page "Runtime: NRT & Kernel Launch" (Instruction fetch mechanics) says that a taken branch to a target outside the fetched window makes the sequencer fetch it by DMA first, and stall. The packets and the place of the wait agree, though no row ties the packets to the five stands in time; where between the two lengths it begins was not tried, beyond that e11 still has it.

- **A record of TensorE with 128 fp32 columns and a load of 128 columns of its own takes 111 ns at full clock** (0.89 us for eight, one behind the other), and 3.58 us for sixteen, twice as much, at the lower level (1095.61 to 1099.19 in the kernel after).
- **An instruction of VectorE can contain a wait for GpSimd**: 3.63 us on average for work of 1.23 (`gate_y`), 5.51 in one case for four elements (`den`, which takes 0.45 on average in e6). The view by groups shows it as busy time, so VectorE's 70% is partly standing.
